# Taking the expert similarities from the unnormalised layer inputs in a four-layer pipeline on one core

## The chip, the core and the metric

The kernel runs on one core of one Trainium2 chip. The metric is device time in microseconds of one execution of the program; smaller is better. The core's engines run side by side, each through its own list of instructions in order: PE (TensorE, matrix products), DVE (VectorE), ACT (ScalarE), POOL (GpSimd) and SP (which here only issues loads and stores). They wait for each other through semaphores.

## What is computed

The input x has 16 sequences ("batches" below) of 512 tokens with 128 features, all float32. Four residual layers follow one another: a selective state-space layer (a), an expert layer, a gated recurrent layer (b), and the same expert layer again. Cut to what matters here:

```
x = x + A(layernorm(x))      # selective scan: 16 states for each of 256 channels, over 512 steps
x = x + FFN(layernorm(x))    # called e1 below; its input is x1
x = x + B(layernorm(x))      # 16-state gated recurrence; input x2
x = x + FFN(layernorm(x))    # called e2 below; its input is x3

def FFN(x):                  # x is the normalised token
    q = x @ w_q              # 2 x 8 heads x 64
    sim = q . keys           # 2 x 8 x 32 similarities for a token
    # best key of each half per head; their sum is the score, their pair is the expert's number
    h = gelu(x . w_down[expert]) * relu(score)
    return sum over the 8 heads of h * w_up[expert]
```

The layer norm before FFN is (x - mean) / sqrt(var + eps), with no weights of its own.

## The kernel before, in words

A token tile has 128 tokens on 128 partitions; a batch is 4 tiles. The program is a software pipeline over the batches. A pass (an "iteration" in the code) is divided into 64 slots. In each pass the core of layer a runs for one batch: 16 recurrence steps on DVE (the scan into `hp`, four slots for each of the 16 states). Around them, in the slots, lie the pieces of other batches: PRE for the next batch, POST for the batches before. POST slots run from 0 to 255, so that a batch's e1 search and gathers lie one pass behind its core, layer b two to three, the e2 search three, the e2 gathers and sums four. Passes -1 to 4 are written out, 5 to 14 are a loop of two passes, and 15 to 19 are written out; 16 to 19 have no recurrence of layer a left and only finish. I call these last four the drain.

The tables `SLOTS` and `LAST_SLOTS` (for passes from 15 on) say in which slot each engine writes each piece. They are no times: they set only the order of instructions on each engine. Where two engines meet is decided by the semaphores.

One expert layer (n = 1 or 2) for one batch goes like this:

- DVE takes mean and variance of x1 or x3 (`statistics`), ACT makes the inverse root (`experts_rstd`), DVE the negative mean times it (`negative_mean`), ACT the normalised tokens `xn` (`experts_norm`).
- PE transposes `xn` into a PSUM bank (`turn`), ACT copies it out to `xnT` (`experts_turned`).
- For each of four tiles t: PE multiplies `xnT` with `w_sim`, the product of query weights and keys that is made once at the start (`experts_sim`); DVE takes the largest of each 32 (`top`) and marks it (`mask`) in `experts_top`. All four go through the same PSUM bank (bank 1 for e1, bank 0 for e2), and `claim` makes PE wait until the bank's last reader is done.
- For each half (two tiles): PE transposes the marks, ACT copies them (`flip`), PE turns them into a code, DVE makes `bits`, `score`, `code` and `index` from it (`experts_index`).
- POOL gathers the experts' rows with one indirect DMA for each head of a tile, 32 for a layer and batch (`fetch`). The first of a half waits for `index` and for the sums of the batch before, which read the same `rows` buffer.
- DVE makes the dots of rows and `xn` (`experts_dot`, L1265), ACT the gelu, DVE the coefficient (L1272), ACT scales the rows (L1005), PE sums them on top of the residual (`experts_sum`, L712 and L716).

POOL also multiplies the states of `POOL_STATES` by c_row (L1479), which PE then adds up (L783). DVE does the others (L1362) and feeds each step (L1336) from b_ps, which PE writes (L758). ACT changes its function table (L933) whenever the next function is not in the loaded set.

Of the kernel before, what the change touches and what calls it, by code (L numbers as in the profile page):

```python
# [5 lines left out]
ALU = mybir.AluOpType  # L6
# [7 lines left out]
P = 128  # L14
# [23 lines left out]
NCR = 1  # L38
# [19 lines left out]
    "pe_turn_x": (PRE, (10,)),  # L58
    "pe_conv": (PRE, (13, 18, 20, 27)),
    "pe_xproj": (PRE, (33,)),  # L60
    "pe_rest": (PRE, (34, 36)),
    "pe_dt": (PRE, (40, 43)),
    "pe_skip": (CORE, (42,)),
    "pe_out": (POST, (2,)),
    "pe_ff1": (POST, (2,)),
    "pe_ff2": (POST, (4,)),
    "pe_ln_a": (POST, (10,)),
    "pe_turn_e1": (POST, (32,)),
    "pe_sim_e1": (POST, (34, 38, 44, 45)),
    "pe_flip_e1": (POST, (42, 48)),  # L70
    "pe_code_e1": (POST, (43, 48)),
    "pe_sum_e1": (POST, (90, 97)),
    "pe_turn_b": (POST, (121,)),
    "pe_xp": (POST, (122,)),
    "pe_gate": (POST, (123,)),
    "pe_y": (POST, (124,)),
    "pe_z": (POST, (140,)),
    "pe_ln_c": (POST, (145,)),
    "pe_turn_e2": (POST, (175,)),
    "pe_sim_e2": (POST, (176, 178, 183, 186)),  # L80
    "pe_flip_e2": (POST, (180, 187)),
    "pe_code_e2": (POST, (182, 189)),
    "pe_sum_e2": (POST, (236, 251)),
    "act_rstd_x": (PRE, (1,)),
    "act_rms_x": (PRE, (2,)),
    "act_keep_x": (PRE, (19,)),
    "act_norm_x": (PRE, (4,)),
    "act_turn_x": (PRE, (9,)),
    "act_conv": (PRE, (17, 20, 27, 28)),
    "act_silu": (PRE, (27, 50)),  # L90
    "act_dbl": (PRE, (33,)),
    "act_soft": (PRE, (39, 41)),
    "act_split": (PRE, (36, 38)),
    "act_exp": (PRE, (50,)),
    "act_ln": (PRE, (56,)),
    "act_out": (POST, (1,)),
    "act_gelu": (POST, (3,)),
    "act_rstd_a": (POST, (7,)),
    "act_rstd_e1": (POST, (22,)),
    "act_norm_e1": (POST, (28,)),  # L100
    "act_turn_e1": (POST, (31,)),
    "act_flip_e1": (POST, (41, 49)),
    "act_gelu_e1": (POST, (67, 82)),
    "act_scale_e1": (POST, (71, 77, 83, 89)),
    "act_out_e1": (POST, (91, 98)),
    "act_rstd_b": (POST, (101,)),
    "act_norm_b": (POST, (119,)),
    "act_turn_b": (POST, (123,)),
    "act_xp": (POST, (125,)),
# [119 lines left out]
def summed(n):  # L229

    return SUM_ORDER.index(n)

# [56 lines left out]
def build(nc, A):  # L289
    with ExitStack() as ctx:  # L290
# [312 lines left out]
        def multiplied(c, n):  # L603

            if n in POOL_STATES:
                return pool_read, at(c, len(POOL_STATES), POOL_STATES.index(n))
# [958 lines left out]
```

## Time and profile before

| | |
|---|---|
| median of 3 runs | 2472.03 us |
| lowest, highest | 2471.53, 2481.04 us |
| span of the profiled execution | 2086.1 us |
| median less span | 385.9 us |
| mean granted TensorE clock | 0.911 of full speed |
| PE, DVE, ACT, POOL busy | 80%, 81%, 75%, 65% of the span |

The span runs from the first to the last instruction that the profile shows. The profiled execution's own device time is not listed beside it, so the 385.9 us are worked out against the median: they lie before and behind the instructions. The shares of busy time are means over a start, a steady part and a drain, which look different.

### The profile page before, as it was taken

What the parts mean: (1) busy time and instruction counts of PE and PEld (TensorE: products, weight loads), DVE (VectorE), ACT (ScalarE), POOL (GpSimd) and SP (SyncE); (2) the same over time, 40 slices, a digit from 0 to 9 for tenths busy, and PEclk for the clock granted to TensorE, in tenths of its full rate; (3) what the DMA queues carried; (4) which work ended last, traced back from release to release, by engine and by line L of the source; (5) the groups of instructions that cost most, each with busy time, mean ns of one, the idle gap of its engine ahead of it and who ended that gap; (6) DMA issues with size and microseconds to landing.
All of it is one profiled execution on the core that took longest, in us unless ns stands there. A gap on an engine that the chain in (4) does not pass through costs nothing. (4 is left out here: it accounts for less than half of the span.)

```text
span 2086.1 us, 24803 instructions
## 1 busy us (share of the span) xinstructions
PE 1665.4 (80%) x6186; PEld 913.5 (44%) x6186; DVE 1683.8 (81%) x4204; ACT 1572.1 (75%) x3300; POOL 1357.9 (65%) x1209
## 2 busy tenths in 40 slices
PE   5778687888898888898888888888889877766653
PEld 2333344444444544454544445444545444344432
DVE  3889888899898989899898989898989988644331
ACT  5556577778888989889888889888888875456443
POOL 0224636376777877776777778776768686767555
PEclk8889899999999999999999999999999998786676
DMA  2001201122323223232323232222323232323222
GB/s 56 11 0 38 63 26 55 33 79 69 89 81 85 83 70 89 71 95 72 89 72 96 71 96 78 81 84 59 103 71 89 66 94 66 91 82 104 77 81 83
DMA packets 79905, 151.09 MB, mean 72 GB/s; under 512 B 20584, under 2 KB 46592, under 8 KB 79680
## 3 DMA queue, kind: packets, MB, share of 16 engines
q0 software_dynamic: 49152, 134.28, 22.6%
q1 hardware_dynamic: 29344, 14.65, 2.5%
q8 instruction: 61, 1.00, 0.2%
q14 instruction: 100, 0.82, 0.1%
q10 hardware_dynamic: 1248, 0.34, 0.1%
HBM read 145.01 MB, written 4.19 MB: 72 GB/s over the span
## 5 line engine op out<-in xcount | busy, mean ns | idle before, releaser
L1464 POOL DMA_INDIRECT rows<-in_experts,index x1024 | 982.5, 959 | 444.5 <-issue 318.0
L1352 DVE TENSOR_TENSOR_SCAN hp<-dA,fed_ps 128x1024 f32<-128x1024 f32 x256 | 583.5, 2279 | 6.4 <-issue 2.4
L783 PE MATMUL ysum<-hp,ident 128*128 128x512 f32 x1024 | 509.6, 645 | 58.0 <-POOL hp L1479 56.6
L1479 POOL TENSOR_TENSOR hp<-hp,c_row 128x1024 f32<-128x1024 f32 x112 | 264.2, 2359 | 256.4 <-ACT c_row L1043 164.1
L1336 DVE TENSOR_TENSOR fed_ps<-du,b_ps 128x1024 f32<-128x1024 f32 x256 | 313.4, 1224 | 66.4 <-PE b_ps L758 44.2
L1026 ACT ACTIVATE dA<-delta,decay 128x511 f32<-128x511 f32 x512 | 335.0, 711 | 25.5 <-issue 16.7
L783 PEld LDWEIGHTS ysum<-hp,ident 128*128 128x128 f32 x1024 | 212.8, 210 | 297.3 <-issue 213.9
L1005 ACT ACTIVATE rows<-rows,coef 128x128 f32<-128x128 f32 x1024 | 310.7, 388 | 13.6 <-DVE coef L1272 13.4
L933 ACT ACT_TABLE_LOAD x242 | 310.5, 1283 | 9.1 <-PEq L543 5.0
L1265 DVE CUSTOM_DVE_ANT_0 rows<-rows,xn 128x128 f32<-128x128 f32 x1024 | 253.4, 312 | 57.9 <-DMA rows<-in_experts,index 57.9
L716 PE MATMUL bank<-rows,ident 128*128 128x256 f32 x1024 | 253.8, 405 | 27.1 <-ACT rows L1005 27.1
L716 PEld LDWEIGHTS bank<-rows,ident 128*128 128x128 f32 x1024 | 211.5, 207 | 62.8 <-ACT rows L1005 29.7
L679 PE MATMUL bank<-w_sim,xnT 128*128 128x512 f32 x256 | 152.8, 681 | 54.9 <-DVE mask L1239 30.8
L1232 DVE TENSOR_REDUCE top<-bank 128x16 f32<-128x512 f32 x128 | 87.8, 686 | 121.8 <-PE bank L679 121.4
L1362 DVE TENSOR_TENSOR hp<-hp,c_ps 128x1024 f32<-128x1024 f32 x144 | 175.0, 1216 | 1.6
L767 PE MATMUL c_ps<-split,pick 128*128 128x512 bf16 x256 | 103.8, 406 | 61.7 <-DVE hp L1362 46.7
L809 PE MATMUL bank<-xrT,w_taps 128*128 128x512 f32 x256 | 118.1, 605 | 2.4 <-ACT ucs L1117 1.5
L998 ACT ACTIVATE x<-bank 128x256 f32<-128x256 f32 x64 | 24.2, 378 | 119.0 <-PE bank L716 118.4
L986 ACT ACTIVATE flip<-bank 128x1024 bf16<-128x1024 bf16 x64 | 65.1, 1018 | 63.0 <-PE bank L690 62.7
L758 PE MATMUL b_ps<-split,pick 128*128 128x512 bf16 x256 | 104.2, 407 | 7.2 <-DVE fed_ps L1336 7.2
L1239 DVE TENSOR_TENSOR mask<-bank,top 128x512 bf16<-128x512 f32 x128 | 88.5, 692 | 13.0
L679 PEld LDWEIGHTS bank<-w_sim,xnT 128*128 128x128 f32 x256 | 44.4, 202 | 95.3 <-DVE mask L1239 43.9
(182 smaller groups left out, 2241.3 us busy)
## 6 DMA issues: line engine op xcount, KB each, us to landing
rows<-in_experts,index POOLq DMA_INDIRECT x1024, 2.8
x_in<-in_x SPq DMA_DIRECT2D x16, 256.0 KB, 4.1
x_res<-in_x SPq DMA_DIRECT2D x16, 256.0 KB, 4.5
y<-x SPq DMA_DIRECT2D x16, 256.0 KB, 2.7
rows<-in_taps SPq DMA_DIRECT2D x1, 512.0 KB
rows<-in_wq_t SPq DMA_DIRECT2D x1, 512.0 KB, 5.3
rows<-in_in_proj_t ACTq DMA_DIRECT2D x1, 256.0 KB
rows<-in_key_t SPq DMA_DIRECT2D x1, 128.0 KB, 5.3
```

What stands on the lines that cost most here:

```text
L679: nc.tensor.matmul(bank[k][:], e.xnT[:, t * P:(t + 1) * P], w_sim[:], start=True, stop=True).then_inc(e.sim, 1)
L716: mm = nc.tensor.matmul(total, ident[:], e.rows[:, tiles, h, P:2 * P], start=False, stop=(h == HEADS - 1), skip_group_check=True)
L783: mm = nc.tensor.matmul(ysum[:, j, :], ident[:], hp[:, BUFFER[k], j, :], start=(k == SUM_ORDER[0]), stop=(k == SUM_ORDER[-1]))
L933: act.preload_act_table_set(name)
L1005: op = nc.scalar.activation(row, row, ACT.Copy, scale=e.coef[:, t, h:h + 1])
L1026: op = nc.scalar.activation(dA[:, n % NDA, j, 1:T], delta[q][:, j, 1:T], ACT.Exp, scale=decay[:, j, n:n + 1])
L1265: op = nc.vector.tensor_tensor_reduce(row, row, e.xn[r][:, t, :], 1.0, 0.0, ALU.mult, ALU.add, e.dot[:, t, h:h + 1])
L1336: nc.vector.tensor_tensor(fed_ps[:], src[:], b_ps[:].to_broadcast([P, NH, T]), ALU.mult).then_inc(fed, 1)
L1352: nc.vector.tensor_tensor_scan(flat, dA[:, n % NDA, :, :].rearrange("p a b -> p (a b)"), fed_ps[:].rearrange("p a b -> p (a b)"), 0.0, ALU ...
L1362: nc.vector.tensor_tensor(state, state, c_ps[:].to_broadcast([P, NH, T]), ALU.mult).then_inc(read_out, 1)
L1464: pool.indirect_dma_start(e.rows[:, t, h, :], None, A["experts"], bass.IndirectOffsetOnAxis(ap=e.index[:, t, h:h + 1], axis=0)).then_inc(e ...
L1479: pool.tensor_tensor(state, state, c_row[:, k % NCR, :].unsqueeze(1).to_broadcast([P, NH, T]), ALU.mult).then_inc(pool_read, 1)
```

## The change

Three things are edited.

1. The similarities are taken from x1 or x3 as they are. PE transposes the layer's input instead of `xn`, and waits for it alone. The mean is taken out in the weights: at the start one more matrix product makes centre x w_sim (centre is the identity less 1/128, which subtracts the mean), and DVE copies it back to `w_sim`. The inverse root is put into the score: one more DVE instruction per half multiplies `score` by `rs`, and waits for `rs`. `xn` is still made, since the dots need it; the first dot of a layer now waits for it itself.
2. The tables `SLOTS` and `LAST_SLOTS` have new numbers in nearly each row.
3. `c_row` loses an index that was always 0, and the split of states between POOL and DVE becomes a function of the batch. `FIRST_BATCHES` is 0, so that it gives the same split as before.

```diff
-    "pe_turn_e1": (POST, (32,)),
-    "pe_sim_e1": (POST, (34, 38, 44, 45)),
+    "pe_turn_e1": (POST, (27,)),
+    "pe_sim_e1": (POST, (35, 37, 44, 46)),
...
-    "dve_top_e2": (POST, (178, 180, 182, 182)),
+    "dve_top_e2": (POST, (178, 180, 182, 184)),
...
-    "pool_fetch_e2": (POST, (201, 201, 208, 211, 211, 212, 212, 220)),
+    "pool_fetch_e2": (POST, (200, 200, 205, 214, 214, 214, 225, 225)),
...
+                self.scored = sem(f"e{n}_scored")
...
                 pe.wait_ge(cleared, 7)
-                nc.tensor.matmul(ysum[:, 1, 2:3], w_gate[:], b_y[:], start=True, stop=True,
-                                 skip_group_check=True).then_inc(folded, 1)
+                nc.tensor.matmul(ysum[:, 1, 2:3], w_gate[:], b_y[:], start=True, stop=True, skip_group_check=True)
+
+                nc.tensor.matmul(bank[1][:], centre[:], w_sim[:], start=True, stop=True).then_inc(folded, 1)
...
                         claim(0, i)
-                        pe.wait_ge(e2.normed, at(m, 1))
-                        turn(0, e2.xn[r], e2.turned)
+                        pe.wait_ge(x3_done, at(m, 1))
+                        turn(0, x3[r], e2.turned)
...
                         claim(1, i)
-                        pe.wait_ge(e1.normed, at(m, 1))
-                        turn(1, e1.xn[r], e1.turned)
+                        pe.wait_ge(x1_done, at(m, 1))
+                        turn(1, x1[r], e1.turned)
...
                 act.wait_ge(e.stats, at(m, 2, 1))
+                if later(m):
+                    act.wait_ge(e.scored, at(m - 1, 2, 1))
...
                 if e.copies == 1 and later(m):
-                    act.wait_ge(e.turned, at(m - 1, 1))
                     act.wait_ge(e.dotted, at(m - 1, NT, NT - 1))
...
                                         ALU.add).then_inc(e.indexed, 1)
+                dve.wait_ge(e.rstd, at(n, 1))
+                nc.vector.tensor_tensor(e.score[:, tiles, :], e.score[:, tiles, :],
+                                        e.rs[:, tiles].unsqueeze(2).to_broadcast([P, HALF, HEADS]),
+                                        ALU.mult).then_inc(e.scored, 1)
 
             def experts_dot(e, r, n, t):
+                if t == 0:
+                    dve.wait_ge(e.normed, at(n, 1))
                 dve.wait_ge(e.fetched[t], (n + 1) * (16 * HEADS))
...
                 dve.wait_ge(folded, 2)
+                nc.vector.tensor_copy(w_sim[:], bank[1][:])
```

The new tables change the order at many places. Three of them matter for what follows.

First place: PE in the last two passes, 18 and 19. bank0 is the bank of e2, x3_0 and x3_1 are the inputs of e2 for batches 14 and 15, rows2 the gathered rows. In the order before, the last batch's transposed input comes first, then the sum of a half of batch 14, and then the first similarities of batch 15:

```order
L662 MATMUL bank0<-ident,xn2_1 128x128 x4
L712 MATMUL bank0<-x3_0,ident 128x256
L716 MATMUL bank0<-rows2,ident 128x256 x8
L679 MATMUL bank0<-w_sim,xnT2 128x512 x2
L690 MATMUL bank0<-ident16,mask2 128x128 x8
L702 MATMUL bank0<-powers,flip2 128x4 x8
L679 MATMUL bank0<-w_sim,xnT2 128x512
L712 MATMUL bank0<-x3_0,ident 128x256
L716 MATMUL bank0<-rows2,ident 128x256 x8
```

and now:

```order
L687 MATMUL bank0<-ident,x3_1 128x128 x4
L704 MATMUL bank0<-w_sim,xnT2 128x512 x2
L715 MATMUL bank0<-ident16,mask2 128x128 x8
L727 MATMUL bank0<-powers,flip2 128x4 x8
L737 MATMUL bank0<-x3_0,ident 128x256
L741 MATMUL bank0<-rows2,ident 128x256 x8
L704 MATMUL bank0<-w_sim,xnT2 128x512 x2
L737 MATMUL bank0<-x3_0,ident 128x256
L741 MATMUL bank0<-rows2,ident 128x256 x8
```

The sum of batch 14's first half has moved behind the two similarities, the transposed marks and the code of batch 15.

Second place: DVE in a pass of the loop, around the second half of the e2 search (top2, mask2: e2; hp<-dA,fed_ps is a recurrence step). Before:

```order
L1248 TENSOR_SCALAR bits2<-bank0 128x32
L1250 TENSOR_TENSOR score2<-top2 128x16
L1253 SCALAR_TENSOR_TENSOR code2<-bits2 128x16
L1257 TENSOR_SCALAR index2<-code2 128x16
L1230 REGISTER_ALU
L1232 TENSOR_REDUCE top2<-bank0 128x16
L1239 TENSOR_TENSOR mask2<-bank0,top2 128x512
L1230 REGISTER_ALU
L1232 TENSOR_REDUCE top2<-bank0 128x16
L1239 TENSOR_TENSOR mask2<-bank0,top2 128x512
L1352 SCALAR_TENSOR_TENSOR hp<-dA,fed_ps 128x1024
```

and now:

```order
L1273 TENSOR_SCALAR bits2<-bank0 128x32
L1275 TENSOR_TENSOR score2<-top2 128x16
L1278 SCALAR_TENSOR_TENSOR code2<-bits2 128x16
L1282 TENSOR_SCALAR index2<-code2 128x16
L1286 TENSOR_TENSOR score2<-score2,rs2 128x16
L1255 REGISTER_ALU
L1257 TENSOR_REDUCE top2<-bank0 128x16
L1264 TENSOR_TENSOR mask2<-bank0,top2 128x512
L1384 SCALAR_TENSOR_TENSOR hp<-dA,fed_ps 128x1024
L1255 REGISTER_ALU
L1257 TENSOR_REDUCE top2<-bank0 128x16
L1264 TENSOR_TENSOR mask2<-bank0,top2 128x512
```

A recurrence step now stands between the third and the fourth largest-of-32, and the multiplication of the score has come in.

Third place: DVE in the same pass, around the first half of the e1 search. Before:

```order
L1232 TENSOR_REDUCE top1<-bank1 128x16
L1239 TENSOR_TENSOR mask1<-bank1,top1 128x512
L1352 SCALAR_TENSOR_TENSOR hp<-dA,fed_ps 128x1024
L1331 REGISTER_ALU
L1336 TENSOR_TENSOR fed_ps<-du1,b_ps 128x1024
L1362 TENSOR_TENSOR hp<-hp,c_ps 128x1024
L1248 TENSOR_SCALAR bits1<-bank1 128x32
```

and now:

```order
L1257 TENSOR_REDUCE top1<-bank1 128x16
L1264 TENSOR_TENSOR mask1<-bank1,top1 128x512
L1363 REGISTER_ALU
L1368 TENSOR_TENSOR fed_ps<-du1,b_ps 128x1024
L1394 TENSOR_TENSOR hp<-hp,c_ps 128x1024
L1273 TENSOR_SCALAR bits1<-bank1 128x32
```

Between the second mark and the reading of the code there was a recurrence step, and now there is none. In the loop's two passes ACT's order holds 32 loads of a function table before and 28 now; in the whole program 242 and 216.

## Rows read from the trace of the kernel before

**Rows 1.** The page: span, and busy time (share of the span) xinstructions of each engine

```profile
span 2086.1 us, 24803 instructions
PE 1665.4 (80%) x6186; PEld 913.5 (44%) x6186; DVE 1683.8 (81%) x4204; ACT 1572.1 (75%) x3300; POOL 1357.9 (65%) x1209
```

**Rows 2.** Busy time by stretch: its us, then PE, PEld, DVE, ACT, POOL, clock, DMA

```profile
558.50:1583.50 1025.00, 887.07 (x3457) 493.42 (x3456) 930.18 (x2342) 892.85 (x1864) 765.83 (x675) 0.96 0.29 82
...
1822.80:2086.10 263.30, 153.25 (x582) 101.01 (x580) 91.10 (x532) 129.26 (x339) 158.79 (x165) 0.73 0.30 85
```

**Rows 3.** Order of time, DVE: first recurrence steps of passes 5 and 14

```profile
558.46 2.28 DVE L1352 TENSOR_TENSOR_SCAN hp<-dA,fed_ps 128x1024 f32<-128x1024 f32 x1
...
1583.49 2.28 DVE L1352 TENSOR_TENSOR_SCAN hp<-dA,fed_ps 128x1024 f32<-128x1024 f32 x1
```

**Rows 4.** DVE's waits, 558.5 to 1583.5: us in total, times, longest

```profile
DVE top L1232 <- PE bank L679: 41.5, 36, 1.9
DVE bits L1248 <- PE bank L702: 10.8, 8, 1.7
DVE fed_ps L1336 <- PE b_ps L758: 9.5, 7, 2.9
```

**Rows 5.** Order of time in pass 10: start, us, [idle before <-releaser]

```profile
1222.40 0.69 DVE L1232 TENSOR_REDUCE top<-bank 128x16 f32<-128x512 f32 x1 [1.75 <-PE bank L679]
...
1225.41 0.69 DVE L1232 TENSOR_REDUCE top<-bank 128x16 f32<-128x512 f32 x1 [1.52 <-PE bank L679]
...
1171.61 6.26 PE L783 MATMUL ysum<-hp,ident 128*128 128x512 f32 x8 [3.77 <-POOL hp L1479]
...
1178.34 1.23 DVE L1336 TENSOR_TENSOR fed_ps<-du,b_ps 128x1024 f32<-128x1024 f32 x1 [2.93 <-PE b_ps L758]
...
1181.05 3.02 DVE L1265 CUSTOM_DVE_ANT_0 rows<-rows,xn 128x128 f32<-128x128 f32 x1
...
1181.55 2.37 POOL L1479 TENSOR_TENSOR hp<-hp,c_row 128x1024 f32<-128x1024 f32 x1
```

**Rows 6.** Groups by line, whole span: busy us, mean ns; or min/median/max ns

```profile
L1250 DVE TENSOR_TENSOR score<-top x64: 161/166/223, 189.6 to 2043.8; 128x16 f32<-128x16 f32 x64
L1272 DVE SCALAR_TENSOR_TENSOR coef<-score,act x64: 160/175/1920, 240.0 to 2072.3; 128x16 f32<-128x16 f32 x64
...
L1265 DVE CUSTOM_DVE_ANT_0 rows<-rows,xn x1024: 257/286/3028, 206.1 to 2071.7; 128x128 f32<-128x128 f32 x171
...
L933 ACT ACT_TABLE_LOAD x242 | 310.5, 1283 | 9.1 <-PEq L543 5.0
L1362 DVE TENSOR_TENSOR hp<-hp,c_ps 128x1024 f32<-128x1024 f32 x144 | 175.0, 1216 | 1.6
```

**Rows 7.** POOL in the drain: first e2 gathers of batches 14 and 15

```profile
1973.76 0.94 POOL L1464 DMA_INDIRECT rows<-in_experts,index  x1 [12.95 <-DVE index L1257]
...
2028.52 0.95 POOL L1464 DMA_INDIRECT rows<-in_experts,index  x1 [13.18 <-DVE index L1257]
```

**Rows 8.** The last batch's e2 search in order of time

```profile
1998.52 1.12 DVE L1222 SCALAR_TENSOR_TENSOR x<-bank,rsC,xnb 128x128 f32<-128x128 f32 x4 [5.27 <-issue]
...
2008.45 0.57 ACT L978 ACTIVATE xnT<-bank 128x512 f32<-128x512 f32 x1
...
2011.41 6.21 PE L716 MATMUL bank<-rows,ident 128*128 128x256 f32 x16 [1.11 <-ACT rows L1005]
...
2018.09 1.13 PE L679 MATMUL bank<-w_sim,xnT 128*128 128x512 f32 x2 [0.47 <-ACT x L998]
...
2022.76 0.69 DVE L1239 TENSOR_TENSOR mask<-bank,top 128x512 bf16<-128x512 f32 x1
...
2027.08 0.19 DVE L1248 TENSOR_SCALAR bits<-bank 128x32 int32<-128x32 int32 x1 [3.63 <-PE bank L702]
```

**Rows 9.** The start: the first copy of w_sim, and the first delta

```profile
43.01 0.69 DVE L1308 COPY w_sim<-bank 128x512 f32<-128x512 f32 x1 [21.52 <-PE ysum L731]
...
45.80 1.23 DVE L1321 TENSOR_TENSOR delta<-delta,du 128x1024 f32<-128x1024 f32 x1 [0.74 <-ACT du L1152]
```

More of the change, by code:

```diff
@@ L37 @@
 NP = 4
-NCR = 1
 BUFFER = [n % NP for n in range(NS)]
@@ new lines @@
+    "act_rms_x": (PRE, (4,)),
+    "act_keep_x": (PRE, (61,)),
+    "act_norm_x": (PRE, (7,)),
+    "act_turn_x": (PRE, (8,)),
+    "act_conv": (PRE, (17, 20, 25, 28)),
+    "act_silu": (PRE, (29, 60)),
+    "act_dbl": (PRE, (35,)),
+    "act_soft": (PRE, (40, 41)),
+    "act_split": (PRE, (36, 38)),
+    "act_exp": (PRE, (42,)),
+    "act_ln": (PRE, (51,)),
+    "act_out": (POST, (2,)),
+    "act_gelu": (POST, (2,)),
+    "act_rstd_a": (POST, (5,)),
+    "act_rstd_e1": (POST, (17,)),
+    "act_norm_e1": (POST, (20,)),
@@ L222, with pool_states, dve_states, sum_at @@
 POOL_STATES = (1, 3, 5, 7, 9, 11, 13)
-DVE_STATES = tuple(n for n in range(NS) if n not in POOL_STATES)
-SUM_AT = [min(n + 1 + (n in POOL_STATES), NS - 1) for n in range(NS)]
-SUM_ORDER = sorted(range(NS), key=lambda n: (SUM_AT[n], n))
-def summed(n):
-    return SUM_ORDER.index(n)
+FIRST_BATCHES = 0
+FIRST_POOL_STATES = tuple(range(14))
+def pool_states(c):
+    return FIRST_POOL_STATES if isinstance(c, int) and c < FIRST_BATCHES else POOL_STATES
+def dve_states(c):
+    return tuple(n for n in range(NS) if n not in pool_states(c))
+def sum_at(c, n):
+    return min(n + 1 + (n in pool_states(c)), NS - 1)
+def sum_order(c):
+    return sorted(range(NS), key=lambda n: (sum_at(c, n), n))
+def summed(c, n):
+    return at(c, NS, sum_order(c).index(n))
+def states_at(c, states, n):
+    if isinstance(c, int):
+        return sum(len(states(b)) for b in range(c)) + states(c).index(n) + 1
+    return states_at(FIRST_BATCHES, states, n) + (c - FIRST_BATCHES) * len(states(c))
 def offset(phase, slot):
@@ L778, in iteration @@
                             pe.wait_ge(y_gated, at(c - 1, 1))
-                        for k in [x for x in SUM_ORDER if SUM_AT[x] == n]:
+                        order = sum_order(c)
+                        for k in [x for x in order if sum_at(c, x) == n]:
                             pe.wait_ge(*multiplied(c, k))
@@ L783, in iteration @@
                                 mm = nc.tensor.matmul(ysum[:, j, :], ident[:], hp[:, BUFFER[k], j, :],
[L784 removed]
+                                                      start=(k == order[0]), stop=(k == order[-1]))
                             mm.then_inc(y_sum, 1)
@@ L1348, in iteration @@
                         if before:
-                            dve.wait_ge(y_sum, at(c, NS, summed(before[-1])))
+                            dve.wait_ge(y_sum, summed(c, before[-1]))
                         elif later(c):
-                            dve.wait_ge(y_sum, at(c - 1, NS, summed(max(k for k in range(NS) if BUFFER[k] == BUFFER[n]))))
+                            dve.wait_ge(y_sum, summed(c - 1, max(k for k in range(NS) if BUFFER[k] == BUFFER[n])))
                         nc.vector.tensor_tensor_scan(flat, dA[:, n % NDA, :, :].rearrange("p a b -> p (a b)"),
@@ L1356, in iteration @@
                         feed(b[CORE], du[q], n + 1)
-                    if CORE in has and part == 2 and n in DVE_STATES:
+                    if CORE in has and part == 2 and n in dve_states(b[CORE]):
                         c = b[CORE]
```

287 lines of the change are left out of this document (134 added, 153 removed).

## The prediction

> **What bounds the kernel now.** I first read the page: DVE has the most busy time, but at 81% of the span no engine is full [rows 1]. A mean over the whole span hides the parts, so I then asked for busy time by stretch. From 558.5 to 1583.5 us lie passes 5 to 13; the reader sees that stretch begin and end with the first recurrence step of a pass [rows 3]. Nine passes take 1025.0 us, 113.9 a pass. In it DVE is busy for 930.2 us (90.7%), ACT for 892.9 and PE for 887.1 (87%), POOL for 765.8 [rows 2]. In the drain, from 1822.8 us, DVE is busy for only 91 of 263 us and POOL for 158.8, and the granted TensorE clock falls to a mean of 0.73, which is part of the time at 1.2 GHz and not 2.4 [rows 2].
>
> So there are two different limits. In the steady part DVE sets the pace: a pass is 103.4 us of DVE work and 10.5 us in which it is not busy. What it waits for there is in the third view, its waits: 41.5 us for PE's similarities (4.6 a pass), 10.8 for PE's codes (1.2 a pass), 9.5 for PE's b_ps (1.05 a pass) [rows 4]. No other engine's work shortens a pass unless it shortens one of these. In the drain it is the latency of one batch's chain, with POOL's gathers as the longest block: 32 gathers for a batch and layer. Before the last two e2 blocks POOL stands still, 12.95 us and 13.18 us, and both times it waits for `index` [rows 7].
>
> **The change part by part.** The profiled execution has a span of 2086.1 us; its own time isn't listed. I take the 385.9 us between it and the median of 2472.0 as fixed, so that every microsecond of span is one of the metric.
>
> *The multiplication of the score* is new on the engine that sets the pace. Its nearest row is the addition of the same 128x16 numbers: 166 ns [rows 6]. Four a pass are 0.66 us. It stands behind `index`, so nothing of the search waits for it; behind it on DVE are the next largest-of-32 and the next recurrence step. Its new wait, for `rs`, I take as nothing: ACT makes `rs` many slots earlier in the new tables. Lower bound 0 (where DVE would have waited for PE anyway), upper bound in the rivals.
>
> *The tables in the steady part.* I go by what stands on DVE between an instruction that PE needs and the one that needs PE.
> - The fourth largest-of-32 of e2 stood straight behind the third's mark, and waited for 1.52 us; the third waited for 1.75 [rows 5]. Now a recurrence step of 2.28 us [rows 3] stands before the fourth, so its wait goes: -1.5 a pass. The third still stands behind `index`, as before: 0.
> - The other 1.3 of the 4.6 us a pass are mostly the first pair of e1. PE and ACT now make the transposed input several slots earlier, and the pair is four slots apart and not one: -1.3.
> - The code of e1's first half: from a mark's end to the reading of the code DVE waited 3.63 us where nothing stood between, with the mark ending at 2023.45 and `bits` starting at 2027.08 [rows 8]. In the new order only a feed (1.23) [rows 5] and a state product (1.22) [rows 6] stand between, some 2.3 us as they overlap a little. That is a new wait: +1.3. Before there was a recurrence step more, and none.
> - The codes of e2: the same chain now has more work ahead of it in the second search pass, and I count half of the 1.2: -0.6.
> - b_ps: in pass 10 PE waits 3.77 us for a state product of POOL, which was held up behind gathers, and 6 us later DVE waits 2.93 us for b_ps [rows 5]. The new table puts a block of three parts at slot 22, behind the product of slot 20, where five parts had stood in slots 16 to 20, so that POOL's products come at their time: -1.05, the whole of this wait.
>
> With the multiplication that is -1.5 - 1.3 + 1.3 - 0.6 - 1.05 + 0.66 = -2.5 a pass, and over the 11 passes from 4 to 14 it is -27 us. Bounds: at best the three waits go altogether, -(4.6 + 1.2 + 1.05) + 0.66 = -6.2 a pass, -68 us; at worst none goes and the new one comes, +2.0 a pass, +22 us.
>
> *ACT's table loads.* Two fewer a pass in the loop, 26 fewer in all, at 1.283 us each [rows 6]: 2.6 us of ACT's time in a pass, 33 us in all. I count nothing. ACT has 132 us without work in the nine passes, and DVE's waits name PE, not ACT [rows 2, 4]. Without DVE as a cover these would be worth up to 2.6 us a pass. The Trainium skill (ScalarE: Activation LUTs, What ACT_TABLE_LOAD costs) gives a switch 2.66 us, with a drain of about 1.38 us beside the load; no row here shows that drain, and by it ACT would be relieved of 5.3 us a pass, which the same cover would hide.
>
> *The start.* A matrix product of 128x512 (1.13 us for its two parts [rows 8]) and a copy (0.69 [rows 9]) come between the first copy of `w_sim` and the first delta. DVE had 0.74 us to wait there for ACT [rows 9], so 1.1 us are left. The multiplications in passes 1 to 3 add 1.2. Together +2.3. Bounds: 0 to 4, where a colder clock doubles the product.
>
> *The drain.* Follow batch 15 [rows 8]. x3 is ready at 1999.6. ACT has the transposed tokens out at 2009.0, because statistics, root, mean and normalising lie between. Then PE does the sum of batch 14's first half, to 2017.6, and the similarities start at 2018.1; the gathers follow at 2028.5 [rows 7], 10.4 us later. In the new order the transposition waits for x3 alone (some 2 us with ACT's copy at 0.57), the search comes first, and `index` would be there at 1999.6 + 2 + 10.4 = 2012.0. Late next is the sum: the gather must not write the rows before batch 14's first half is summed, and that now stands behind batch 15's code. With 6.2 us for the sum and 1.2 for the residual ahead of it, it ends at 2019.4: 9 us earlier than 2028.5. POOL's 12.95 us before batch 14's gathers go the same way in part, but only as far as layer b of batch 15 gets its x3 earlier by it; I count 5. Together -14. Bounds: both of POOL's gaps closed, -26; nothing, where x3 itself comes later because the new order puts more sums and searches ahead of layer b, 0.
>
> Sum: -27 + 2 - 14 = -39; 2472.0 - 39 = 2433.
>
> **The rivals.**
>
> *A: the two-input instructions on DVE meet POOL's products (slower).* A dot on DVE took 3.02 us while POOL multiplied a state, from 1181.55 to 1183.92, against a median of 0.286; the coefficient, also of 128x16 with both inputs in SBUF, has a maximum of 1.92 us against a median of 0.175 [rows 5, 6]. The multiplication of the score is of that kind. Against it: the addition that stands three instructions ahead of it never took more than 0.223 us in 64 times [rows 6]. If each of the four a pass met a product and lost 1.2 us more, that is 4.8 us a pass, 72 us over 15 passes, and the time is 2433 + 72 = 2505. It ends on the slower side from 52 us on, so when about 7 in 10 meet one, or fewer if dots that used to miss the products are now hit too. The Trainium skill (SBUF — State Buffer, Who interferes with whom) states the rule: a DVE instruction with both inputs in SBUF and a GpSimd instruction that reads SBUF exclude each other for the whole instruction. The trace agrees with that rule, with the 3.02 us above.
>
> *B: the waits only move (same).* The tables leave DVE's 6.8 us a pass of waits as they are, since PE keeps one bank a layer; the multiplication costs 0.66 x 15 = 10 and the start 1, the drain gives 14. That is 2469. For it: each of the eight searches still goes through PE and back, and PE is busy for 87%.
>
> *C: the drain and the steady part both give more.* PE's lateness is the common cause of DVE's waits, and with ACT lighter it falls away: -4.5 a pass (-50), both of POOL's gaps closed (-26), start +2: 2398. For it: two thirds of DVE's 10.5 us are waits for PE. Against it: DVE and PE were both near 90%, and two such engines in lockstep rarely get that close.
>
> *D: the order of some engine is simply worse* in a few passes (a wait for `rs` or for x_in at a pass's start, since the normalising that frees x_in goes from slot 19 to slot 61): some 3 us a pass against me, 2433 + 45 = 2478. It has part of the chance of the slower side.
>
> **How the numbers follow.** My forecast has 0.57, with its own range of 2412 to 2452; C 0.17; B 0.14; A and D 0.12 together. The range that leaves 2 in 10 outside reaches from C's 2398 to 2476, past B and to the edge of D. A difference under 0.5% (12.4 us) is about what a measurement of this kernel can't tell from none. Forecast and C are faster by more: 0.74; B is within: 0.14; A and D slower: 0.12.
>
> **What would show it.** The same nine passes (first recurrence step of pass 5 to that of pass 14) should take about 1003 us and not 1025. DVE's wait for PE's similarities there should fall from 41.5 to below 20 us, and that for codes should stay near 10, since one goes and one comes. The multiplications should have a median near 0.166 us and few above 1. POOL's wait before the last block of gathers should be under 6 us. ACT's table loads should be 216. I am wrong if the nine passes take 1025 or more (B, D), if the multiplications or dots have many members above 1 us (A), or if the drain is as long as its 263 us.

## The result, and the profile after

The changed kernel is slower: 2496.6 us in the median of 12 runs against 2473.3 us of the kernel before in 12, a ratio of 1.0087, 95% interval 1.0061 to 1.0112. I had forecast 2433 us, 2398 to 2476. The median is 20 us above the range, on the other side of no change.

One thing must be known before any row is read. The times come from six occasions, each on one chip, and the same kernel before takes 2471 to 2473 us on three of them, 2388 on one and 2088 to 2089 on two. In every other profiled execution the span is 1.7 to 1.8 us shorter than its time, so the one of before, with its span of 2086.1 us [rows 1], must be of the last kind, and the median that I set it against was of the first. So I profiled the changed kernel again where the kernel before takes 2089.4 us. The ratio there is 1.0212 (1.0180 to 1.0243), the profiled execution 2128.7 us with a span of 2126.9. All rows of after in this section are from it, and they can be held against the rows of before one to one. The page:

```profile
span 2126.9 us, 24883 instructions
PE 1659.6 (78%) x6188; PEld 909.6 (43%) x6188; DVE 1816.0 (85%) x4269; ACT 1541.6 (72%) x3274; POOL 1362.3 (64%) x1209
```

The two first recurrence steps that bound the nine passes, and busy time in them and in the drain (its us, then PE, PEld, DVE, ACT, POOL, clock, DMA):

```profile
555.73 2.28 DVE L1384 TENSOR_TENSOR_SCAN hp<-dA,fed_ps 128x1024 f32<-128x1024 f32 x1
...
1645.44 2.28 DVE L1384 TENSOR_TENSOR_SCAN hp<-dA,fed_ps 128x1024 f32<-128x1024 f32 x1
```

```profile
555.70:1645.40 1089.70, 902.10 (x3457) 498.77 (x3456) 1029.51 (x2377) 871.20 (x1846) 767.26 (x673) 0.92 0.27 76
1879.10:2126.90 247.80, 141.78 (x586) 94.86 (x584) 90.98 (x525) 122.40 (x334) 163.21 (x170) 0.77 0.33 95
```

Against [rows 2] the reader sees the whole case. Nine passes take 1089.7 us and not 1025.0. DVE is not busy for 60.2 us of them instead of 94.8, so the waits did shrink. But it is busy for 1029.5 us instead of 930.2, though it runs only 35 instructions more. The drain is 15.5 us shorter. The span splits as: first step of pass 0 2.6 us later, passes 0 to 4 5.4 shorter, the nine passes 64.7 longer, passes 14 and 15 5.6 shorter, the drain 15.5 shorter. Together +40.8, the difference of the spans.

DVE's waits in the nine passes, to be held against [rows 4]:

```profile
DVE bits L1273 <- PE bank L727: 23.5, 18, 2.2
DVE top L1257 <- PE bank L704: 7.9, 14, 0.7
...
DVE fed_ps L1368 <- PE b_ps L784: 4.3, 10, 0.6
```

Where the busy time came from stands in DVE's groups of the same nine passes (busy us, mean ns of one):

```profile
L1296 DVE CUSTOM_DVE_ANT_0 rows<-rows,xn 128x128 f32<-128x128 f32 x576 | 174.0, 364 | 0.0
...
L1275 DVE TENSOR_TENSOR score<-top 128x16 f32<-128x16 f32 x36 | 42.9, 1191 | 0.0
L1286 DVE TENSOR_TENSOR score<-score,rs 128x16 f32<-128x16 f32 x36 | 25.6, 711 | 0.0
...
L1303 DVE SCALAR_TENSOR_TENSOR coef<-score,act 128x16 f32<-128x16 f32 x36 | 16.8, 466 | 0.0
```

In the kernel before, the same groups had in its nine passes 7.1 us for the coefficient, and for dots and addition:

```profile
L1265 DVE CUSTOM_DVE_ANT_0 rows<-rows,xn 128x128 f32<-128x128 f32 x576 | 137.7, 304 | 0.2 <-DMA rows<-in_experts,index 0.2
...
L1250 DVE TENSOR_TENSOR score<-top 128x16 f32<-128x16 f32 x36 | 6.1, 169 | 0.0
```

The multiplication (L1286) is new. The addition of 128x16 numbers went from 169 ns to 1191 in the mean, with not one number more to add. Its median is still 167 ns: a few members are very long. What they stand beside is seen in the order of time, here at the code of the first half of e2 in pass 10, behind recurrence step 13 (DVE and POOL; PE's next similarities):

```profile
1255.61 2.37 POOL L1511 TENSOR_TENSOR hp<-hp,c_row 128x1024 f32<-128x1024 f32 x1
1255.92 0.19 DVE L1273 TENSOR_SCALAR bits<-bank 128x32 int32<-128x32 int32 x1 [2.17 <-PE bank L727]
1256.03 4.28 DVE L1275 TENSOR_TENSOR score<-top 128x16 f32<-128x16 f32 x1
1257.91 2.35 POOL L1528 TENSOR_TENSOR delta<-delta,du 128x1024 f32<-128x1024 f32 x1
1260.23 0.16 DVE L1278 SCALAR_TENSOR_TENSOR code<-bits 128x16 f32<-128x16 int32 x1
1260.42 2.38 POOL L1532 TENSOR_TENSOR du<-delta,ucs 128x1024 f32<-128x1024 f32 x1 [0.16 <-POOL delta L1528]
1260.43 0.17 DVE L1282 TENSOR_SCALAR index<-code 128x16 uint32<-128x16 f32 x1
1260.51 2.33 DVE L1286 TENSOR_TENSOR score<-score,rs 128x16 f32<-128x16 f32 x1
1260.66 2.07 PE L704 MATMUL bank<-w_sim,xnT 128*128 128x512 f32 x2 [4.28 <-DVE index L1282]
```

Read POOL's and DVE's rows against each other. The addition starts under POOL's product of a state and ends at 1260.31, when the product of delta behind it ends too (1260.26). The code starts as POOL's second product ends, the index 0.01 us behind the start of the third, and both are short. The new multiplication starts 0.09 us after the product of du and ends 0.04 us after it. PE may use the bank again only behind the index, and it waits 4.28 us. That is 6.3 us of DVE's time at one place, and it happens in each of the nine passes.

From here on "excess" is this: for each DVE instruction that overlaps a product or an addition of POOL and is clearly longer than the median of its group, what it is longer by, summed over the nine passes. It is 10.5 us in the kernel before and 118.2 us here: addition after recurrence step 13 36.9 (9 members), multiplication there 19.4 (9), dots after step 8 24.5 and after step 5 17.3, the rest below 9 each. The difference of 107.7 us is more than DVE's 99.3 more of busy time, in which rows that overlap count once.

45 of DVE's instructions in these nine passes were held for more than 1 us, and each of them ends 0.02 to 0.16 us after a product or addition of POOL ends. By the records 9 of them start up to 0.5 us before POOL's instruction does, and are held all the same. In the same passes 36 statistics (one input), 9 of DVE's own state products (one input in SBUF, one in PSUM) and 9 readings of a code from PSUM lay wholly inside a product of POOL, and none was longer for it.

Which instruction is caught depends on the chip. In the changed kernel's first profiled execution (2494.9 us, of the kind of the median) the excess is 104.1 us, nearly as much, but after step 13 it lies on the code (25.7, 5 members), the index (10.1), the addition (9.9) and the dots (7.6), and the multiplication has 4.3; the dots after step 5 have 19.3.

### The profile page after: what moved, and what is told of

It is laid out like the page before. It is cut to its first block and busy times, and to the rows that moved or that the text cites. A ratio compares the mean times of both kernels' runs of the same rounds, so it can differ in the third digit from the quotient of the medians.

```text
span 2493.1 us, 24795 instructions
## 1 busy us (share of the span) xinstructions
PE 1769.4 (71%) x6100; PEld 965.4 (39%) x6188; DVE 1790.5 (72%) x4269; ACT 1547.5 (62%) x3274; POOL 1354.1 (54%) x1209
## 5 line engine op out<-in xcount | busy, mean ns | idle before, releaser
L810 PE MATMUL ysum<-hp,ident 128*128 128x512 f32 x1024 | 533.5, 667 | 85.3 <-DVE hp L1394 68.6
L810 PEld LDWEIGHTS ysum<-hp,ident 128*128 128x128 f32 x1024 | 222.5, 219 | 336.0 <-issue 236.7
L1054 ACT ACTIVATE dA<-delta,decay 128x511 f32<-128x511 f32 x512 | 334.6, 711 | 16.3 <-issue 14.0
L1033 ACT ACTIVATE rows<-rows,coef 128x128 f32<-128x128 f32 x1024 | 310.2, 390 | 13.3 <-DVE coef L1303 12.9
L1296 DVE CUSTOM_DVE_ANT_0 rows<-rows,xn 128x128 f32<-128x128 f32 x1024 | 270.1, 325 | 20.6 <-DMA rows<-in_experts,index 16.6
L704 PE MATMUL bank<-w_sim,xnT 128*128 128x512 f32 x256 | 176.9, 783 | 75.4 <-DVE index L1282 42.3
L1026 ACT ACTIVATE x<-bank 128x256 f32<-128x256 f32 x64 | 24.5, 382 | 311.0 <-remote 194.5
L784 PE MATMUL b_ps<-split,pick 128*128 128x512 bf16 x253 | 112.9, 446 | 54.1 <-DVE fed_ps L1368 42.7
L1069 ACT ACTIVATE c_row<-c_ps 128x512 f32<-128x512 f32 x112 | 65.8, 587 | 104.8 <-remote 51.3
L793 PE MATMUL c_ps<-split,pick 128*128 128x512 bf16 x173 | 74.1, 428 | 51.1 <-DVE hp L1394 23.5
L704 PEld LDWEIGHTS bank<-w_sim,xnT 128*128 128x128 f32 x256 | 54.3, 238 | 116.4 <-DVE index L1282 46.3
```

The source lines that it names most:

```text
L704: nc.tensor.matmul(bank[k][:], e.xnT[:, t * P:(t + 1) * P], w_sim[:], start=True, stop=True).then_inc(e.sim, 1)
L810: mm = nc.tensor.matmul(ysum[:, j, :], ident[:], hp[:, BUFFER[k], j, :], start=(k == order[0]), stop=(k == order[-1]))
L1033: op = nc.scalar.activation(row, row, ACT.Copy, scale=e.coef[:, t, h:h + 1])
L1054: op = nc.scalar.activation(dA[:, n % NDA, j, 1:T], delta[q][:, j, 1:T], ACT.Exp, scale=decay[:, j, n:n + 1])
L1296: op = nc.vector.tensor_tensor_reduce(row, row, e.xn[r][:, t, :], 1.0, 0.0, ALU.mult, ALU.add, e.dot[:, t, h:h + 1])
```

## The experiments

Ratios are to the kernel before on the same chip at the same time, with the 95% interval; the number in brackets is what the kernel before took there.

**Is the profiled execution of before one that the median is made of?** The kernel before, unchanged, once more.

> The kernel before, unchanged, for a second profiled execution. In the changed kernel the span is 1.7 us shorter than the time in every run. Theory: that holds for the kernel before too, so its span is about 2470 us, the nine passes 5 to 13 take about 1250 us (139 each) and not 1025, and the execution with a span of 2086.1 us, from which I predicted, was not one of those that the median is made of. Rival: the span is near 2086 again and some 386 us lie outside it.

A single run: time 2400.4, span 2398.6 (2388): 1.8 us lie outside the span, and nine passes take 1193.8 us. The theory holds, with smaller numbers than I gave, since this chip is of a third kind.

```profile
582.90:1776.80 1193.90, 927.10 (x3456) 506.24 (x3456) 926.12 (x2342) 891.88 (x1863) 766.32 (x676) 0.91 0.25 70
```

DVE's and ACT's busy time are those of [rows 2] within 4 us; what grew by 173 us is the time in which DVE waits. PE is busy for 40 us more, at a mean granted clock of 0.91 and not 0.96. So "385.9 us outside" was wrong. The profile was a true one, of a chip on which the kernel takes 2088.

**Which part of the change costs?** Three kernels with one or two of its three parts (arithmetic, main table, last table):

```diff
 e_math:       new arithmetic,  SLOTS of before,  LAST_SLOTS of before
 e_slots_math: new arithmetic,  SLOTS of after,   LAST_SLOTS of before
 e_slots:      old arithmetic,  SLOTS of after,   LAST_SLOTS of before
```

> The changed kernel with both of its tables of slots put back to those of before: only the new arithmetic (similarities from the inputs, multiplication of the score by the inverse root, two table loads fewer a pass, the product at the start). Theory 'tables': the arithmetic costs only its four multiplications of 0.17 us a pass and the start, and saves ACT table loads, so the time is within 8 us of before (2466 to 2482). Rival 'arithmetic': the multiplications on DVE, when they meet POOL's products, or the root that waits, cost the 23 us, so the time is 2490 to 2500 here too. Multiplications and dots over 1 us would be many more than in the kernel before.

> The changed kernel with the table of the last batches put back to that of before; the main table and the arithmetic are the new ones. Theory 'main table': the loss is in the passes, the time stays near 2496 and the drain differs by less than 10 us. Rival 'last table': the loss is in the drain, so the time falls to about 2473.

> The kernel before with the main table of the changed kernel alone; the arithmetic and the table of the last batches are those of before. Theory 'main table': the time is 2485 to 2500, as the new order makes DVE's two-input instructions meet more of POOL's products. Rival 'arithmetic': the order does nothing by itself, within 8 us of 2473, and the loss needs the multiplications.

All (2388): e_math 1.0038 (1.0011 to 1.0065), 9 us, about what the multiplications at their median and the start would cost (0.66 x 15 + 1 = 11, an estimate; its nine passes, 1190.7 us, don't show it); its excess is 8.8 us. e_slots_math 1.0193 (1.0155 to 1.0232); e_slots 1.0197 (1.0153 to 1.0240). The main table alone brings the loss, with the old arithmetic too. The nine passes of e_slots, to hold against those of b_again just above:

```profile
573.30:1808.50 1235.20, 961.70 (x3449) 520.62 (x3450) 1015.07 (x2341) 874.49 (x1843) 765.31 (x675) 0.88 0.24 68
```

DVE without work: 220.1 us against 267.8. DVE busy: +89. Excess: 103.6 against 6.1. DVE waits 47.7 us less, so 97.5 us more of excess come out as 41 us of time. The largest part is 30.5 us of the index, which meets the row of POOL's products in six passes. The row of that group over the whole span (min/median/max ns):

```profile
L1257 DVE TENSOR_SCALAR index<-code x64: 174/174/5303, 183.2 to 2377.1; 128x16 uint32<-128x16 f32 x64
```

This instruction has one input, so it was not in my rival A. The Trainium skill (SBUF — State Buffer, Who interferes with whom) lists tensor_scalar among the operations that can take the pair of ports shared with GpSimd, under conditions that no run here tests; the 5.30 us agree with that.

**The changed kernel where before takes 2089, and one number of it put back.**

> The changed kernel, unchanged, beside the next three on one chip, so that it can be set against the run with the last batches' table of before (1.0193, 95% 1.0155 to 1.0232). Theory: the ratio is 1.009 again, so the new last table alone gives back about 1% (25 us), in the last two stretches (pass 15 and the drain). Rival: the two earlier sessions differ, and here the ratio is 1.015 to 1.02, so the last table gives nothing.

1.0212 (2089). The expectation took the difference to e_slots_math as the worth of the last table; the ratio of the unchanged changed kernel is itself 1.009 on some chips and 1.021 on others, so ratios of different chips can't be subtracted. What the last table gives is seen only in the drain above, -15.5 us, and only on this kind of chip: where the kernel before takes 2471 to 2473, the changed kernel's drain is 356.8 us and, in a_ref2 below, 351.6, against 346.0 in b_late below, which has the last table of before.

```diff
-    "pool_delta": (PRE, (53,)),
+    "pool_delta": (PRE, (51,)),
```

> The changed kernel with one number put back: POOL's two products of delta stand at slot 51 as before, not at 53, where the product of state 13 comes first and the three stand in a row. In the nine passes of the changed kernel a search instruction of DVE stood 5 us against this row in nearly every pass: 52 us of the 104 by which DVE's instructions were longer than their medians there. Theory 'lock at scan 13': those members over 2 us go, and the time falls by 30 to 60 us over 11 passes, so to a ratio of 0.985 to 0.997 to before. Rival 'the wait only moves': the search instruction is shorter, but DVE or PE waits elsewhere for what was late anyway, and the ratio stays within 0.3% of the changed kernel's.

1.0125 (1.0090 to 1.0159) (2089). Half right: 16 us and not 30 to 60. Excess 93.8 against 118.2 (24.4 less), nine passes 1065.7 us against 1089.7 (24.0 less). Here a microsecond of excess is a microsecond of time; it is no rule, as a_nomul and a_dots below show. More than half of the excess after step 13 stays.

**Take the meetings away altogether.** In both kernels POOL's large products work on 8 of 128 columns; the rest of these products is left out.

```diff
-                        state = hp[:, BUFFER[n], :, :]
+                        state = hp[:, BUFFER[n], :, 0:8]
```

> The kernel before with POOL's large products cut to 8 of 128 columns (state products, delta, du); the rest of these products is left out, nothing else changes. It is the ground for the next run. POOL's 2.36 us products become about 0.3 us. Theory 'lock': in this kernel DVE loses only 6 us to them in nine passes, so what it gains is only what DVE and PE waited for POOL's result, 1 to 4% of the time.

> The changed kernel with the same cut of POOL's large products. Theory 'lock': the 104 us of excess in nine passes fall below 15, and this kernel is faster than the kernel before with the same cut, by 30 to 80 us (its DVE waits are 48 us shorter in nine passes). Rival 'order': the new placement costs time by itself, and it is 15 us or more slower than the kernel before with the same cut.

0.9702 (0.9661 to 0.9742) and 0.9389 (0.9350 to 0.9427) (2089): 2025.7 and 1960.2 us. Nine passes of the changed one, then of the one before:

```profile
527.50:1503.40 975.90, 862.73 (x3458) 482.52 (x3457) 918.80 (x2377) 869.75 (x1846) 596.29 (x676) 0.98 0.30 86
```

```profile
532.90:1531.20 998.30, 876.46 (x3457) 487.56 (x3456) 918.75 (x2342) 891.00 (x1864) 590.33 (x676) 0.98 0.30 84
```

Without the meetings (excess 7.0 and 0) DVE is busy for the same 918.8 us in both, and the changed kernel is 65 us faster: 22.4 us of it in the nine passes, 2.5 a pass, and 38 behind them (passes 14 and 15, and the drain). Against the changed kernel with whole products, DVE's busy time is 110.7 us less of the 113.8 that the nine passes lose, so it is the holding that goes and not a wait for POOL's results. The 2.5 a pass equal my sum, but in part by luck: the waits for sims, codes and b_ps that I had counted give 1.4 of it.

**The multiplication, and other rows of the table.** The reference, and the factor left out:

```diff
-                nc.vector.tensor_tensor(e.score[:, tiles, :], e.score[:, tiles, :], ... ALU.mult).then_inc(e.scored, 1)
+                dve.sem_inc(e.scored, 1)
```

> The changed kernel unchanged again, as the reference for the next three on their chip: the kernel before took 2472, 2388 and 2089 us in the three sessions so far and the ratio was 1.0087 in the first and 1.0212 in the third. Theory: where the kernel before takes about 2090 us the ratio is 1.02, where it takes about 2400 or more it is 1.01. Rival: the ratio has nothing to do with that.

> The changed kernel without the multiplication of the score by the inverse root; that factor is left out. Theory 'lock as a whole': the multiplication's own members beside POOL's product of du cost 2.2 us a pass and the other 27 of 36 only 0.17 us, but DVE's block behind them stands at the same product, so taking it away gives back 10 to 30 us, not the whole loss, and the ratio to before stays above 1.005. Rival 'the multiplication is the loss' (rival A as I put it, 4.8 us a pass): the ratio falls by 0.03 to 0.99.

1.0208 (1.0177 to 1.0238) and 1.0153 (1.0126 to 1.0180) (2088): 11 us of the 45, as expected. The excess goes from 119.7 to 103.0 only, since two others now meet products (L1448, which makes m from m and rs, 13.1 us, and the coefficient after step 5, 12.9). And what DVE is busy for less (17.7 us) it waits more in the profiled execution (78.8 us and not 58.0, mostly for sims). The multiplication is not the loss.

```diff
-    "dve_dot_e2": (POST, (212, 224, 228, 238)),
+    "dve_dot_e2": (POST, (210, 221, 226, 236)),
```

> The changed kernel with the slots of DVE's dots of the second expert layer put back to those of before (210, 221, 226, 236 and not 212, 224, 228, 238). In the changed kernel each of the nine passes had one dot of about 2.5 us after scan 8 and one after scan 5, beside POOL's products of states 7 and 5: 42 us of the 118 us of excess. Theory 'lock': these members go, and the ratio falls by 0.010 to 0.025. Rival 'wait moves': the dots are short but come before their rows have landed or push the recurrence, and the ratio falls by less than 0.004.

1.0280 (1.0254 to 1.0306) (2088): against my expectation slower by 0.7%. The dots after step 8 are short now, and the coefficient stands in their place in every pass (25.3 us, 9 members), dots of other groups meet the addition to x (14.5) and the row after step 13 (39.4); the excess is 120.0, as in the changed kernel, and the nine passes are 13.9 us longer because DVE is without work for 71.3 us and not 58.0. The coefficient in pass 10, and POOL's product, which by the records starts 0.55 us after it and ends 0.05 us before it:

```profile
1224.62 2.97 DVE L1303 SCALAR_TENSOR_TENSOR coef<-score,act 128x16 f32<-128x16 f32 x1
...
1225.17 2.37 POOL L1511 TENSOR_TENSOR hp<-hp,c_row 128x1024 f32<-128x1024 f32 x1
```

```diff
 as a_dots, and
-    "pool_delta": (PRE, (53,)),
+    "pool_delta": (PRE, (57,)),
```

> As the run before it, and POOL's two products of delta go from slot 53 to slot 57, behind the first block of gathers of the first expert layer and not in front of it, so that DVE's search code is over when they run. Theory 'lock': the 56 us of excess after scan 13 in nine passes shrink below 15, the dots' too, and the ratio to the kernel before is 0.97 to 0.99: faster than both kernels. Rival 'the chain of delta': the products of delta feed the next pass's first decays and first feed, they now come 5 us later, and what DVE saves it waits for there; the ratio is 1.00 or more.

1.0049 (1.0031 to 1.0068) (2088): 2.3% below a_dots. Excess 78.7 against 120.0, nine passes 1057.8 us against 1102.9. Not the 0.97 to 0.99 that I expected: the dots were still in their bad place, and 23 us of excess stay after step 13, where I had said below 15.

**A version that should beat both.** The changed kernel with pool_delta at 57 (a_late), also with POOL's two additions at 4 and 140 as before (a_late_x), and the kernel before with pool_delta at 57 (b_late).

> The changed kernel with the products of delta at slot 57 and nothing else (dots as in the changed kernel). In nine passes the excess was 118 us; 56 of it stood after scan 13. So far each us of excess taken away was 1.0 to 1.1 us of time (24 for 24, 41 for 45). Theory 'meetings': excess near 65, nine passes near 1035 us, ratio to the kernel before 0.985 to 0.997. Rival: the next two-input instruction meets the product of state 13 or the moved ones instead, as when the dots were moved, excess stays above 90 and the ratio above 1.005.

> The same, with POOL's two additions to x_res and x also back at the slots of before (4 and 140, not 8 and 144). In the changed kernel 15 us of the excess stand beside them. Theory 'meetings': up to 15 us less in nine passes than the run before it, ratio lower by 0.003 to 0.008. Rival: they meet others there, no difference over 0.003.

> The kernel before with the products of delta at slot 57 and not 51. Its excess is only 10 us in nine passes, so there is nothing to take away. Theory 'meetings': no gain; within 0.4% of the kernel before, or slower, as the products come behind four gathers (5 us) and feed the next pass. Rival 'slot 57 is good by itself' (the gathers start earlier): 0.5 to 2% faster.

0.9810 (0.9775 to 0.9846), 0.9699 (0.9646 to 0.9752) and 1.0063 (1.0039 to 1.0086) (2472). Excess 63.3, 53.9 and 13.3. Both are faster than the kernel before, and by a little more than I expected (0.985 to 0.997, and 0.003 to 0.008 from the one to the other). b_late is no clean control: in its order the late slot puts the products of delta behind 16 gathers and not 4, and they start 33 us after step 13 and not 13. It shows that this slot is worth nothing in the old order, and not why it pays in the new one.

**Why did the products of delta meet the search only in the new order?**

```diff
-    "act_ln": (PRE, (51,)),
+    "act_ln": (PRE, (56,)),
```

> The changed kernel with ACT's logarithm for the next batch's delta back at slot 56 (new: 51). In the kernel before, in pass 10, DVE's second search code of the first expert layer was over at 1220.65 us and ACT's logarithm ended at 1221.99, so POOL's products of delta, which wait for it, came after the search. In the changed kernel the logarithm ends at 1247.82, and the products stand ready 8 us before POOL reaches them, straight behind the product of state 13 and in the middle of the search code. Theory: the late logarithm kept the two apart, and putting it back takes most of the 56 us after scan 13 away; ratio 0.010 to 0.025 below the changed kernel's beside it. Rival: the order on POOL alone decides (product of state 13, then delta), and the ratio changes by less than 0.005.

> The changed kernel unchanged, as the reference beside the other two. 1.009 if the kernel before takes about 2470 us here, 1.021 if it takes about 2090.

> The version with delta's products at slot 57 and the two additions at 4 and 140 again, beside the changed kernel on one chip. It had 0.970 where the kernel before took 2472 us. Theory: it is 0.03 or more below the changed kernel whatever the kernel before takes, so 0.975 to 0.99 where that is about 2090 us. Rival: the gain belongs to the chips where the kernel before is slower, and it is 1.0 or more where it takes 2090.

a_ln 0.9983 (0.9950 to 1.0016), a_ref2 1.0087 (1.0055 to 1.0119), a_late_x2 0.9739 (0.9701 to 0.9777), all (2471). One number of ACT's, and the loss is gone: 1.0% below the changed kernel beside it, excess 62.9 against 104.3, and after step 13 24.7 against 58.0. POOL now waits for the logarithm in each of the nine passes (4.4 to 6.6 us), and the search code is over when it starts:

```profile
1248.86 2.34 POOL L1528 TENSOR_TENSOR delta<-delta,du 128x1024 f32<-128x1024 f32 x1 [5.25 <-ACT du L1177]
```

The expectation has one thing wrong: the code that was over at 1220.65 us is that of e2's first half. And the logarithm holds POOL back in the old order only on some chips. In b_again POOL waits for it in each of the nine passes (3.7 to 5.8 us); in the execution of 2086.1 us it never does, since the logarithm has ended 0.5 to 1.6 us before POOL is through with its gathers. There it is the gathers ahead of delta's products that keep them behind the search.

The last run gives the best version 3.5% less than the changed kernel on the same chip. Not all of that is meetings: the nine passes are 88 us shorter than in a_ref2 for 49 us less of excess. DVE is busy for 36 us less and without work for 52 less; in a_ref2 77.5 us of waits stand ahead of DVE's state products, 9 of them, whose releaser the trace does not name. Why they went stays open. Whether the best version keeps its lead where the kernel before takes 2088 us was not measured; a_d57, with its dots in a bad place, was 1.6% below the changed kernel there.

## Why the prediction was wrong

**The step that failed** is rival A, which I had right as a mechanism and dismissed as a risk ("Against it: the addition that stands three instructions ahead of it never took more than 0.223 us in 64 times"; A and D 0.12 together). The row is true, but it is a row of the old order. It said that this addition did not meet a product in the old placement, and the change was a new placement. In the new one it met two in a row in every pass, 4.28 us at a time, and the multiplication behind it the third. I had priced A at 4.8 us a pass and thought of the multiplication. The excess rose by 107.7 / 9 = 12.0 us a pass, of which the multiplication has 2.2; in my sum the meetings stood at nothing. "Or fewer if dots that used to miss the products are now hit too" was the sentence that should have had the weight. Nothing in my sum asked of a moved DVE instruction beside which POOL product it would now stand.

**The waits** I had about right in the sum, partly by luck. Sims, codes and b_ps fell from 61.8 us to 35.7, 2.9 a pass; my terms without the multiplication are 3.15. Single terms were off both ways. The sims' wait is 7.9 us and not just below 20; part of that seems to be only that DVE is held while PE works, for without the meetings, in a_small, it is 16.3. The codes' wait is 23.5 where I said about 10. The new wait of e1's first code is 0.50 us a pass and not 1.3, and the code of e2's first half, which I had better by 0.6, is worse by 0.8: 2.1 us a pass, 2.17 in the rows of pass 10 above. b_ps gave 0.6 a pass, not 1.05. DVE's time without work fell by 34.6 us, 3.8 a pass.

**The multiplication** at its median costs 0.169 us, 0.68 a pass, nearly as put; 11 of 64 were over 1 us.

**ACT's table loads** are 216, as forecast, and gave nothing that can be seen: ACT was busy for 21.7 us less in the nine passes and the passes are longer. But one move in ACT's order was not free of effect, and this I had not looked for: its logarithm is earlier, and where the kernel before takes 2471 that brings POOL's products to the search (a_ln).

**The start** came 2.6 us later, of which I had 1.1: DVE's first product of delta starts at 48.42 us and not at 45.80 [rows 9]. DVE waits 2.71 us for PE's product. The 1.13 us of [rows 8] are both its parts at a granted clock of 1.00; at the start the clock is 0.50, and they take 2.05:

```profile
45.36 2.05 PE L766 MATMUL bank<-w_sim,centre 128*128 128x512 f32 x2
```

That was in my bounds, not in my term.

**The drain** is 15.5 us shorter; I had 14. The first gathers of e2 for batches 14 and 15, to be held against [rows 7]:

```profile
2028.06 0.94 POOL L1496 DMA_INDIRECT rows<-in_experts,index  x1 [8.35 <-PE bank L741]
...
2069.95 0.94 POOL L1496 DMA_INDIRECT rows<-in_experts,index  x1 [0.99 <-issue]
```

12.95 became 8.35, now for PE's sum of the batch before: 4.6 us less, where I counted 5. 13.18 became 0.99, under the 6 that I named as the sign. From batch 15's x3 (ready at 2050.54) to its first gather it is 19.4 us, as in my chain (2019.4 less 1999.6, 19.8), and not 28.9. What I had not counted is the wait ahead of batch 15's e1 gathers: 12.75 us before the first half, and now 4.45 before the first and 5.05 before the second. POOL's waits ahead of these blocks fall by 21 us in all and the drain by 15.5, so that 14 comes near is partly luck. And it holds on this kind of chip alone: in the execution of 2494.9 us POOL stands for 33.67 and 31.44 us at the same two gathers, and the drain is no shorter.

**The 385.9 us** were no constant. They were the difference of two kinds of chip, whose waits differ, and I read the terms of one and added them to the time of the other. They did not decide the sign: where the kernel before takes 2089 the change costs 2.1%, where it takes 2472, 0.9%.

So the sum of -39 had -27 for the passes 4 to 14, and what came was +7.2 a pass: -3.8 of waits, +0.66 of the multiplication, +12.0 of meetings, the rest (-1.7) mostly that neighbouring rows of DVE overlap by more (164.3 us in all and not 155.1, 1.0 a pass).

## What to carry to other kernels

When a table of slots moves work, list for each large GpSimd product which DVE instructions with two SBUF inputs (and which tensor_scalar) stand within its length in the new order, or up to 0.5 us ahead of it, and price each meeting at what is left of the product, or of the whole row of products. The price is not yet the time: part of it can come back as shorter waits (e_slots), and part of a repair can be lost to longer ones (a_nomul). "It never took long" in the old trace says only where it stood. Work moved earlier on one engine can bring another engine's work forward into a collision; look at what the released work will stand beside. And set a profiled execution against the median only after its own time is known.

## What the runs showed of the hardware

On the chip on which the kernel before takes 2388 us, DVE and ACT only wait more: their busy time is the same to 1% (1676.4 and 1571.8 us in b_again, against [rows 1]). PE is busy for 1720.0 us against 1665.4, at a mean granted clock of 0.862 against 0.911. One of the stops, in b_again: eight transposes of PE at the full clock (granted 1.00) are over at 1348.99, and ACT, which needs only them, starts 4.3 us later:

```profile
1348.38 0.61 PE L690 MATMUL bank<-ident,mask 128*128 128x128 bf16 x8
...
1353.33 1.02 ACT L986 ACTIVATE flip<-bank 128x1024 bf16<-128x1024 bf16 x1 [5.12 <-remote]
```

"remote" means that the trace holds no event that released it. ACT's waits ahead of this copy are 75.4 us in nine passes there, and 22.8 in the execution of 2086.1 us. The granted clock falls only at 1353.2, when the stop is over. A stop of 5 to 7 us at this copy is in each of the nine passes, and each overlaps gathers of POOL. I have no experiment on its cause, and it stays open. What excess is worth seems to depend on the chip too: 41 us of it less in nine passes went with 24 us of time between a_ref2 and a_ln (2471), and with 51 us between a_dots and a_d57 (2088). These are two different edits, so that is not shown.
